# A GRU and a mixture of experts in one kernel: input part and bias seeded into PSUM by ACT, the two halves summed in one DVE op

## The reference

```python
def cell(h, x):
    gi = x @ W_ih + b_ih
    gh = h @ W_hh + b_hh
    r = sigmoid(i_r + h_r)
    z = sigmoid(i_z + h_z)
    n = tanh(i_n + r * h_n)
    h_new = (1.0 - z) * n + z * h
scores = einsum('btd,ed->bte', states, Wg)      # top 2, softmax over the two
y = sum_e w[..., e] * ((silu(s @ W1[e].T) * (s @ W2[e].T)) @ W3[e].T)
out = x + y
```

## Time and profile before

| | |
|---|---|
| median of 3 runs | 1649.89 us |
| the profiled execution | 1657.09 us |
| its span | 1655.4 us |
| TensorE busy | 1445.0 us, 87% |
| DVE busy | 1124.0 us, 68% |
| ACT busy | 671.5 us, 41% |
| POOL busy | 406.9 us, 25% |
| the chain that ended last | PE 63%, DVE 14%, DMA 8%, issue 7%, ACT 4% |

### The profile page before, as it was taken

One profiled execution on the slowest core, in us unless ns is written; L12 is line 12 of the kernel. 1 busy time (PEld: TensorE's weight loads), 2 busy tenths in 40 slices (PEclk: granted clock), 3 DMA queues, 4 the chain that ended last, 5 costly groups with the idle time before them and its releaser, 6 DMA issues.

```text
span 1655.4 us, 69764 instructions
## 1 busy us (share of the span) xinstructions
PE 1445.0 (87%) x29785; PEld 1175.7 (71%) x29785; DVE 1124.0 (68%) x4419; ACT 671.5 (41%) x1564; POOL 406.9 (25%) x857
## 2 busy tenths in 40 slices
PE   4678776699999999999999999999999888766676
PEld 4677665588888888887888878788888777534343
DVE  4588676777777787777777777777777777512221
ACT  5264453234434444444344444344444333333333
POOL 1001221022222222222222222222222222422213
PEclk9788887699999999999999999999999888778988
DMA  8747454434544454445444444444444444568764
GB/s 284 237 155 208 126 141 150 177 111 143 168 143 143 143 168 143 143 143 166 135 143 142 154 140 145 125 140 135 145 146 144 143 143 144 163 203 255 241 204 142
DMA packets 93734, 265.71 MB, mean 161 GB/s; under 512 B 33007, under 2 KB 50415, under 8 KB 83312
## 3 DMA queue, kind: packets, MB, share of 16 engines
q1 hardware_dynamic: 75472, 227.60, 42.0%
q0 software_dynamic: 17952, 33.64, 8.9%
HBM read 217.47 MB, written 55.79 MB: 165 GB/s over the span
## 4 chain that ended last, share of the span: by engine, by line
PE 63%; DVE 14%; DMA 8%; issue 7%; ACT 4%; POOL 2%; SPq 2%; another core or an unknown queue 1%; DVEq 0%; POOLq 0%; ACTq 0%
PE gn_bank L1063 10%; PE gz_ps L1063 9%; PE b_ps L1084 9%; PE y_ps L1147 6%; PE a_ps L1110 6%; PE b_ps L1110 5%; PE gr_ps L1049 5%; PE gr_ps L1055 5%; PE gi_ps L1084 5%; DMA mt<-meta 3%; DMA work<-h_tok,mt 3%; DVE zpre L850 2%; DVE hn L850 2%; DMA out_y<-work,mt 2%; PE tr_ps L1124 1%
## 5 line engine op out<-in xcount | busy, mean ns | idle before, releaser
L1063 PE MATMUL gn_bank<-hlog,whh 128*128 128x32 f16 x8192 | 246.7, 177 | 7.5 <-issue 7.5
L1063 PE MATMUL gz_ps<-hlog,whh 128*128 128x32 f16 x8192 | 247.1, 177 | 4.8 <-issue 4.4
L535 POOL DMA_INDIRECT out_y<-work,mt x71 | 115.4, 1626 | 525.5 <-ACT work L721 359.0
L1049 PEld LDWEIGHTS gr_ps<-hlog,whh 128*128 128x128 f16 x4096 | 125.9, 97 | 155.2 <-DVE hlog L882 106.0
L1063 PEld LDWEIGHTS gn_bank<-hlog,whh 128*128 128x128 f16 x8192 | 225.2, 96 | 8.2 <-issue 8.1
L1063 PEld LDWEIGHTS gz_ps<-hlog,whh 128*128 128x128 f16 x8192 | 225.5, 96 | 5.6 <-issue 5.6
L1049 PE MATMUL gr_ps<-hlog,whh 128*128 128x16 f16 x4096 | 143.2, 170 | 98.7 <-DVE hlog L882 84.8
L1084 PE MATMUL b_ps<-x_split,wih 128*128 128x512 f32 (+1 forms) x792 | 199.5, 398 | 0.0
L1147 PE MATMUL y_ps<-wbuf,work 128*128 128x512 f16 x639 | 172.2, 405 | 1.8 <-ACT work L698 1.8
L1110 PE MATMUL a_ps<-wbuf,work 128*128 128x352 f16 x852 | 150.7, 330 | 24.9 <-issue 24.9
L675 ACT ACTIVATE nt<-npre 128x64 f32<-128x64 f32 x256 | 65.7, 257 | 247.9 <-DVE npre L869 231.9
(11 more groups left out here) (161 smaller groups left out, 2312.4 us busy)
## 6 DMA issues: line engine op xcount, KB each, us to landing
wbuf<-wscr SPq DMA_DIRECT2D x71, 1410.0 KB, 6.6
wbuf<-wscr SPq DMA_DIRECT2D x71, 768.0 KB
h_tok<-xrow SPq DMA_DIRECT2D x32, 256.0 KB
x_raw<-in_x_feat SPq DMA_DIRECT2D x7, 1024.0 KB, 5.0
wscr<-wbuf SPq DMA_DIRECT2D x9, 768.0 KB, 4.5
wscr<-wbuf SPq DMA_DIRECT2D x9, 706.0 KB, 4.5
wscr<-wbuf SPq DMA_DIRECT2D x9, 704.0 KB, 4.0
work<-in_w_units SPq DMA_DIRECT2D x8, 512.0 KB
```

What stands on the lines that cost most here:

```text
L535: pool.indirect_dma_start(out=out, out_offset=bass.IndirectOffsetOnAxis(ap=mt[:, j % RING, 0:1].bitcast(I32), axis=0), in_=ysc[:, j % 2], ...
L1049: pe.matmul(gr_ps[:, j, 0], whh[:, 1, k, j * P:(j + 1) * P], h[:, k, 0], start=(j == 0 and k == 0), stop=False, skip_group_check=True)
L1063: mm = pe.matmul(dst[:, j], whh[:, i, k, m * P:(m + 1) * P], h[:, k], start=(k == 0 and i == 0), stop=(k == K - 1 and i == 1))
```

## The change

A gate's bank is filled ahead of its matmuls: ACT writes the input part (r and z) or the bias (n), times `SC_SEED`, into both halves of the bank. `SC_SEED` is 0.5 times the product of the scales of the weights and of the state, so that the two halves together give the value at the scale of the matmuls. All matmuls of `recur` then add to what stands there (`start=False`), and DVE sums the two halves with one `tensor_reduce` a gate. The inverse scale moves into the scale of the sigmoids and into npre, which becomes a scalar_tensor_tensor; the sigmoid of z takes the negative scale, so zs is 1 - z, and the new state is h + zs x (n - h), a plain addition. Before the first seeds, TensorE writes one matmul with `start=True` into each of the three banks (`gates_open`). The seeds of step t+1 are issued by ACT in step t: that of r after the sigmoid of r, that of n after hn, that of z after the sigmoid of z; where step t+1 begins a chunk, those of r and z come after the step's `take_piece`. TensorE waits for each seed before the gate's first matmul.

```diff
+        SC_SEED, SC_MINUS = 10, 11
-        N_BIAS, N_MAGS, N_SETUP = 2, 22, 37
+        N_BIAS, N_MAGS, N_SETUP = 2, 22, 39
# ACT
+            def seed(gh, values, seeded):
+                S.activation(gh[:], values.unsqueeze(2).to_broadcast([P, K, 2, B]), ACT.Copy,
+                             scale=scale(SC_SEED)).then_inc(seeded, 1)
+            def gi_of(t, gate):
+                c, at = t // STEPS, t % STEPS * B
+                if t % STEPS == 0:
+                    act.wait_ge(gi_taken, HEAD if t == 0 else piece_no(c + 1, 0))
+                if t == STEPS // 2:
+                    act.wait_ge(gi_taken, 2 * HEAD)
+                return gi[:, c % 2, gate * K:(gate + 1) * K, at:at + B]
             def gru_acts(t):
-                act.wait_ge(gru_ops, gru(t, "R_B"))
-                S.activation(rs[:], rpre[:, 1], ACT.Sigmoid).then_inc(sig_r, 1)
+                act.wait_ge(gru_ops, gru(t, "R"))
+                S.activation(rs[:], rpre[:], ACT.Sigmoid, scale=scale(SC_INV)).then_inc(sig_r, 1)
+                if t + 1 < T and (t + 1) % STEPS:
+                    seed(gr_ps, gi_of(t + 1, 0), r_seeded)
+                act.wait_ge(gru_ops, gru(t, "HN"))
+                if t + 1 < T:
+                    seed(gn_ps, bhn[:], n_seeded)
                 act.wait_ge(gru_ops, gru(t, "N_PRE"))
                 S.activation(nt[:], npre[:], ACT.Tanh).then_inc(tanh_n, 1)
-                act.wait_ge(gru_ops, gru(t, "Z_B"))
-                S.activation(zs[:], zpre[:, 1], ACT.Sigmoid).then_inc(sig_z, 1)
+                act.wait_ge(gru_ops, gru(t, "Z"))
+                S.activation(zs[:], zpre[:], ACT.Sigmoid, scale=scale(SC_MINUS)).then_inc(sig_z, 1)
+                if t + 1 < T and (t + 1) % STEPS:
+                    seed(gz_ps, gi_of(t + 1, 1), z_seeded)
...
+            act.wait_ge(setup, N_SETUP)
+            act.wait_ge(gates_open, 1)
+            seed(gr_ps, gi_of(0, 0), r_seeded)
+            seed(gn_ps, bhn[:], n_seeded)
+            seed(gz_ps, gi_of(0, 1), z_seeded)
...
                 for n, i in G_AT[t]:
                     if i == pieces[n].halves - 1:
                         take_piece(n)
+                if t + 1 < T and (t + 1) % STEPS == 0:
+                    seed(gr_ps, gi_of(t + 1, 0), r_seeded)
+                    seed(gz_ps, gi_of(t + 1, 1), z_seeded)
# DVE
-                def add(dst, gh, half, base):
-                    op(V.scalar_tensor_tensor(out=dst, in0=gh[:, :, half, :], scalar=inv, in1=base,
-                                              op0=ALU.mult, op1=ALU.add))
+                def halves(dst, gh):
+                    op(V.tensor_reduce(dst, gh[:].rearrange("p k a b -> p k b a"), AX_X, ALU.add))
-                add(rpre[:, 0], gr_ps, 0, gi_r)
-                after("R_A")
-                add(rpre[:, 1], gr_ps, 1, rpre[:, 0])
+                halves(rpre[:], gr_ps)
...
-                op(V.tensor_tensor(npre[:], rh[:], gi_n, ALU.add))
+                op(V.scalar_tensor_tensor(out=npre[:], in0=rh[:], scalar=scale(SC_INV), in1=gi_n,
+                                          op0=ALU.mult, op1=ALU.add))
...
-                    op(V.scalar_tensor_tensor(out=dst, in0=nt[:], scalar=scale(SC_H), in1=znh[:],
-                                              op0=ALU.mult, op1=ALU.subtract))
+                    op(V.tensor_tensor(dst, h_now[:, now], znh[:], ALU.add))
# DVE, setup
+            chain(V.tensor_scalar(scale(SC_SEED), scale(SC_W), 0.5, scale(SC_H), ALU.mult, ALU.mult))
+            chain(V.tensor_scalar(scale(SC_MINUS), scale(SC_INV), -1.0, None, ALU.mult))
# TensorE
+                pe.wait_ge(r_seeded, t + 1)
-                                  start=(j == 0 and k == 0), stop=False, skip_group_check=True)
+                                  start=False, stop=False, skip_group_check=True)
...
-                for dst, first in ((gn_ps, 2 * K), (gz_ps, K)):
+                for dst, first, seeded in ((gn_ps, 2 * K, n_seeded), (gz_ps, K, z_seeded)):
+                    pe.wait_ge(seeded, t + 1)
...
-                                               start=(k == 0 and i == 0), stop=(k == K - 1 and i == 1))
+                                               start=False, stop=True, skip_group_check=True)
...
+            pe.wait_ge(setup, N_MAGS)
+            for gh in (gr_ps, gn_ps, gz_ps):
+                mm = pe.matmul(gh[:].rearrange("p k a b -> p (k a b)"), ident[:], ident[:], start=True, stop=True)
+            mm.then_inc(gates_open, 1)
```

More of the change, by code:

```diff
@@ L143, in gru_moe_kernel @@
             in_bank[pieces[b[1]].bank] = b[1] + 1
-    GRU = "R_A R_B HN_A HN_B R_HN N_PRE Z_A Z_B N_H Z_NH H_HI H_NEW H_LO".split()
+    GRU = "R HN R_HN N_PRE Z N_H Z_NH H_HI H_NEW H_LO".split()
     FFN = "GATE HID MAG EXP UP_SCALE DOWN_SCALE HID_LO".split()
@@ L193, in gru_moe_kernel @@
         hlog = sb("hlog", [P, 2, K, 2, P], F16)
-        rpre = sb("rpre", [P, 2, K, B])
-        zpre = sb("zpre", [P, 2, K, B])
+        rpre = sb("rpre", [P, K, B])
+        zpre = sb("zpre", [P, K, B])
         rs = sb("rs", [P, K, B])
         zs = sb("zs", [P, K, B])
-        hn1 = sb("hn1", [P, K, B])
         hn = sb("hn", [P, K, B])
@@ L313, in gru_moe_kernel @@
         gi_taken = sem("gi_taken")
+        gates_open = sem("gates_open")
+        r_seeded = sem("r_seeded")
+        n_seeded = sem("n_seeded")
+        z_seeded = sem("z_seeded")
         gh_ready = sem("gh_ready")
@@ L838, in gru_step @@
                 gi_t = gi[:, c % 2, :, at:at + B]
-                gi_r, gi_z, gi_n = gi_t[:, 0:K], gi_t[:, K:2 * K], gi_t[:, 2 * K:M]
-                inv = scale(SC_INV)
+                gi_n = gi_t[:, 2 * K:M]
                 parts = h_parts(t)
@@ L857, in gru_step @@
                 dve.wait_ge(gh_ready, 3 * t + 1)
-                add(rpre[:, 0], gr_ps, 0, gi_r)
-                after("R_A")
-                add(rpre[:, 1], gr_ps, 1, rpre[:, 0])
+                halves(rpre[:], gr_ps)
                 dve.wait_ge(gh_ready, 3 * t + 2)
-                add(hn1[:], gn_ps, 0, bhn[:])
-                after("HN_A")
-                add(hn[:], gn_ps, 1, hn1[:])
+                halves(hn[:], gn_ps)
                 dve.wait_ge(sig_r, t + 1)
-                after("HN_B")
+                after("HN")
                 op(V.tensor_tensor(rh[:], rs[:], hn[:], ALU.mult))
                 after("R_HN")
-                op(V.tensor_tensor(npre[:], rh[:], gi_n, ALU.add))
+                op(V.scalar_tensor_tensor(out=npre[:], in0=rh[:], scalar=scale(SC_INV), in1=gi_n,
+                                          op0=ALU.mult, op1=ALU.add))
                 dve.wait_ge(gh_ready, 3 * t + 3)
-                add(zpre[:, 0], gz_ps, 0, gi_z)
-                after("Z_A")
-                add(zpre[:, 1], gz_ps, 1, zpre[:, 0])
+                halves(zpre[:], gz_ps)
                 dve.wait_ge(tanh_n, t + 1)
```

## The result

| | before | after |
|---|---|---|
| median of 5 runs each, one chip | 1649.89 us (1648.02 to 1651.82) | 1635.34 us (1628.76 to 1637.48) |
| ratio | | 0.9904, 95% 0.9884 to 0.9925 |
| profiled execution, span | 1657.09, 1655.4 us | 1635.34, 1633.6 us |
| TensorE, DVE, ACT busy | 1445.0, 1124.0, 671.5 us | 1432.9, 923.8, 926.1 us |

The medians differ by 14.6 us, 19.6 were forecast for them; the profiled executions differ by 21.8 us.

What follows compares the result with a forecast made beforehand. TensorE was taken to bound the long middle, with idle gaps early and late. Savings of 28.9 us less 8.4 at boundaries and 0.9 at the start gave 19.6, so 1649.9 became 1630 us, range 1617 to 1648.

Steps and rivals of the forecast that it cites:

- Start: Before the first recurrent matmul: two more setup ops and the first seed with its hand-over add 0.9 us.
- Early: Steps 0 to 47: shorter chain saves 11.1 us in late-DVE gaps and 3.0 in ordinary ones; step 32's boundary costs 0.6.
- The rival that took the whole early gain for lost: Weight loads and preparation set the pace in steps 0 to 47, so 14.1 us is lost: 1644; chance 0.17.
- The step that gave nothing to four gaps: Steps 21 to 24 and 36 to 39: DVE waits for POOL's maximum, so gains before the wait are lost: 0.
- Boundaries: At chunk starts TensorE waits for seeds needing the last piece: six at 1.3 us, 7.8, plus 0.6 at step 32.
- Middle, the rest: Steps 48 to 225 apart from boundaries: the shorter chain returns 5.8 of 6.3 us of TensorE's waits for hlog.
- Late: Steps 226 to 255: four gaps of 0.37 in full, four late-DVE at 0.84, seven ordinary at 0.60, saving 9.0 us.
- the rival that had the clock come back: Shorter gaps keep TensorE at 2.4 GHz, saving 4.8 us late and a similar 4 early: 1621; chance 0.17.
- Costs at nothing: TensorE's added waits for seeds and ACT's added work, some 238 us in total, were priced at no time.
- the rival at 1668: Each gate's first weight load, 768 times, loses 50 ns to its new wait, 38 us in all; chance 0.08.
- The dear reduction: Each gate's DVE reduction takes 0.57 us, like the two ops it replaces, leaving 5.7 us saved: 1644; chance 0.07.
- The absolute time: Whole kernel: profiled execution 1657.09 to 1637.5 us; the same 19.6 us saving from the median 1649.9 gives 1630.

Runs made afterwards that it cites:

- second profiles: The kernel before and the kernel after, each unchanged, profiled once more: 1666.43 us for before, 0.9917 of before for after.
- early seeds: Against the kernel after, r and z seeds of a chunk's first step issued in their usual places, waiting only for the pieces they read: 0.9844 of before.
- the kernel with all three edits: Against the kernel after: boundary seeds in usual places, POOL's appends two steps later until step 40, reordered start; 1622.66 us, 0.9750 of before.

## Why the prediction was right

The forecast fell 5.3 us below the measured median, and its mechanism, the shorter chain in the steps where TensorE waits for it, is the measured one. That the sum came so close is partly luck: the middle gave more than forecast for a reason that the forecast did not have, while the late stretch and step 31 gave less; the tail from step 255 on, 1.9 us longer in this pair of profiles and 1.3 shorter in the second, was not in it. By its own steps, in the first profiles of the two kernels:

*Start:* +0.9 forecast, +1.46 measured (44.87 to 46.33; +1.07 in the second profiles). The two setup ops moved DVE's last one by 0.95, and the seed with its hand-over took 0.5.

*Early:* -14.1 + 0.6 forecast, -12.6 measured. The savings of the gaps are there. So is the absorption in front of POOL: step 24 grew from 9.83 to 12.48 us and step 39 from 18.37 to 19.15. With POOL's appends moved the early stretch gains 4 us more in the profiles. The rival that took the whole early gain for lost (1644) is refuted. The step that gave nothing to four gaps is near: steps 21 to 24 and 36 to 39 gave back 3.1 us together, most of what went into the wait for POOL having been gained just ahead of it.

*Boundaries:* six at 1.3 forecast, 7.8; six at 1.42 measured, 8.5. At step 32 0.6 was forecast and step 31 grew by 3.1 us (8.18 to 11.32). Two things are in it. TensorE's wait for the seed is 1.2, twice the term; the rest is idle time of TensorE inside the n gate with no wait beside it, 4.5 us, where before had 2.6 inside the z gate of the same step:
```profile
229.43 0.32 PE L1092 MATMUL gn_bank<-hlog,whh 128*128 128x32 f16 x6 [4.49 <-issue]
```
It is there with early seeds too (5.1 us in the kernel with all three edits, but 1.2 in the one with that edit alone, which so gained some 3 us by chance). What ends it is open.

*Middle, the rest:* -5.8 forecast, -15.8 in the first pair of profiles, and -13.1 between the means of two profiles each, from different chips; with the 9 us between the two profiles of after, this is a size and not a measurement to a us. The term is the most mis-sized all the same. Its step priced only what the table put down to hlog (6.3 us), and that by the length of the chain. Of the two-profile figure 7.6 us stand in steps 8k+5, where DVE had waited in front of the z gate for TensorE's late increments while POOL's appends ran, and where the kernel after has none. The forecast did not look at who DVE waited for there, a row that the profile of before had; but that the change would rid the kernel of late increments could not be had from its mechanism, and to that part the gain is luck: kernels with the same short chain and early boundary seeds have 63 and 64 of them.

*Late:* -9.0 forecast, -5.2 measured. Step by step: eleven ordinary steps gave 0.43 to 0.48 each, 4.9; four late-DVE ones 0.70 to 0.83, 2.9; the fourteen others lost 2.65 together. The first two sums are near their terms (5.7 and 3.4); the last is not in the forecast. It stands in steps 241 and 249, 1.7 and 0.9 longer, where TensorE has idle time inside a gate that before has not:
```profile
1331.46 0.28 PE L1092 MATMUL gn_bank<-hlog,whh 128*128 128x32 f16 x5 [1.53 <-issue]
```
The steps with group A gave nothing in sum (39.7 and 39.8 us): some of these groups fell to half rate (3.35, 3.44 and 3.68 us for 12 matmuls, 2.6 to 3.0 in before), others ran at full rate (1.95). The granted clock rose from 0.86 to 0.92 in this stretch all the same, so part of the rival that had the clock come back is there, without the gain of 4.8 us that it was given. The Trainium skill (TensorE: Matmul & The Clock Gate, Part 1: The HAM clock gate) has idleness halve the clock; the trace has half-rate spells behind gaps, but filling the gaps didn't end them.

*Costs at nothing:* TensorE's waits for the n and z seeds: starts still 25 ns apart, no row of such a wait, and the middle shrank; the rival at 1668 is refuted. The idle time under "issue" that grew stands inside the gates, not in front of a gate's first matmul, where the new waits are. ACT's load: 0.9977 with it alone.

*The dear reduction* (1644): refuted by 289 ns. By the rule of the Trainium skill (Advanced Engine Details and Errata, PSUM Cachelines) the strided pairs would have been slower than neighbours; against the slope of the earlier trace rows, whose reductions read SBUF, they were not. No run has neighbouring pairs in PSUM beside them.

*The absolute time:* the difference of the profiled executions was 21.8 for 19.6, that of the medians 14.6. Before's profiled execution was 7.2 above its median and after's lay on it, so the step from the one to the other carried over a difference that was partly that execution's.

## What to carry to other kernels

Price a shorter chain gap by gap, each with the smaller of gap and saving, and ask of every other wait that stands before a gap whether it began from an earlier moment: such a wait swallows what is gained ahead of it, and moving its cause (here one number in POOL's order, 18 us) can be worth more than the change. When an operand is prepared ahead, let it wait for exactly the part that it reads; the coarse wait for a whole chunk cost 10 us here. Read who the helper engine waits for, not TensorE alone: the largest miss stood in a row of DVE's waits. And where such a row names no clear releaser, look up when the semaphore moved before blaming the engine that waits; here it was TensorE's increment that came late. To judge a shorter chain, compare single steps that have no other stall: the ordinary late ones agree to 0.02 us over the profiles of before, and over those of after, while whole stretches differ by 9 us.

## What the runs showed of the hardware

- A scale read from a column costs ACT 0.09 us on 64 elements: 346 and 348 ns against 255 and 257 with a constant, the same ops otherwise.
- ACT wrote 128 elements into PSUM in 0.352 to 0.364 us; the same form of op into SBUF took 0.391.
- DVE summed 128 fp32 of PSUM, in pairs 16 elements apart, in 289 ns; two ops on 64 took 219 to 223 and 225 ns.
- In eight of the 14 profiles TensorE's semaphore increments came up to 2.4 us late while POOL's indirect transfers (mostly 1.0 to 1.7 us each) ran, 31 of the 53 that fell into one in before; in the other six none of those did, 0 of 88 in after.
